# Depthwise 1/3/5 convolution with projection and residual on one core: the set-up of weights and statistics is dealt out anew among the engines

## The reference

```python
xd = concatenate([x[:, :, 0::2, 0::2], x[:, :, 0::2, 1::2], x[:, :, 1::2, 0::2], x[:, :, 1::2, 1::2]], axis=1)  # (8,128,32,32)
feats = concatenate([dwconv(xd, w1, 1), dwconv(xd, w3, 3), dwconv(xd, w5, 5)], axis=1)                       # depthwise, (8,384,32,32)
y = einsum('bchw,oc->bohw', feats, w_proj)            # 384 -> 128 channels, then back to 32 channels of 64x64
# the whole: x + conv(group_norm(x)), with 32 groups of one channel each
```

## Time and profile before

| | |
|---|---|
| median of 3 runs | 139.71 us (139.51 to 141.06) |
| profiled execution, whole | 139.66 us |
| profiled execution, span from first to last instruction | 137.8 us |
| busy PE, DVE, ACT, POOL | 92%, 90%, 79%, 85% of the span |
| granted TensorE clock, mean | 0.99 |

### The profile page before, as it was taken

How to read it: one execution, slowest core, us unless ns; L and a number is a source line. 1 busy time by engine, 2 the same in 40 slices (tenths; PEclk the granted TensorE clock), 3 DMA queues, 4 the chain that set the end, 5 groups by cost and what they waited for, 6 DMA issues and landing times.

```text
span 137.8 us, 1549 instructions
## 1 busy us (share of the span) xinstructions
PE 126.6 (92%) x508; PEld 94.8 (69%) x508; DVE 123.9 (90%) x152; ACT 109.1 (79%) x111; POOL 117.6 (85%) x88
## 2 busy tenths in 40 slices
PE   5896999999999999999999999999999999999620
PEld 5673787877876777777786777687767678577300
DVE  6659799999999999999999999999999999999660
ACT  2259989999999999999999999999999995140000
POOL 6261899999999999999999999999999999999500
PEclk9999999999999999999999999999999999999996
DMA  3999999971025008098988957795779577496596
GB/s 75 273 259 197 195 204 201 182 148 20 2 57 105 0 2 164 5 112 133 193 102 94 190 110 76 76 189 125 76 76 186 128 76 76 87 153 69 116 201 140
DMA packets 35847, 16.78 MB, mean 122 GB/s; under 512 B 34048, under 2 KB 34176, under 8 KB 35456
## 3 DMA queue, kind: packets, MB, share of 16 engines
q0 software_dynamic: 1488, 7.04, 38.0%
q1 hardware_dynamic: 32720, 9.18, 35.8%
q10 hardware_dynamic: 1632, 0.48, 1.8%
HBM read 5.46 MB, written 4.19 MB: 70 GB/s over the span
## 4 chain that ended last, share of the span: by engine, by line
DVE 76%; PE 12%; DMA 3%; issue 3%; ACT 1%; DVEq 1%; ACTq 0%
DVE ACC L602 48%; PE YP L675 10%; DVE ACC L606 7%; DVE ACC L594 7%; DVE F L612 6%; DVE st L492 3%; DMA wp_sb<-in_L_conv_w_proj_dram 3%; PE YP L726 1%; DVE weff L543 1%; DVE stp L498 1%; ACT HI L387 1%; DVEq L97 1%; ACT weff L379 1%; DVE X L636 0%; PE YP L657 0%
## 5 line engine op out<-in xcount | busy, mean ns | idle before, releaser
L317 POOL TENSOR_TENSOR RING_SUM<-RING_SUM,PROD 128x900 f32<-128x900 f32 (+1 forms) x45 | 92.6, 2065 | 3.4
L602 DVE SCALAR_TENSOR_TENSOR ACC<-G,coef,ACC 128x930 f32<-128x930 f32 (+1 forms) x59 | 70.4, 1194 | 1.8
L435 ACT ACTIVATE PROD<-G,coef 128x900 f32<-128x900 f32 (+1 forms) x45 | 44.7, 1057 | 0.0
L675 PE MATMUL YP<-HI,wlo 128*128 128x512 f32 (+1 forms) x144 | 38.3, 419 | 0.0
L675 PE MATMUL YP<-HI,whi 128*128 128x512 f32 (+1 forms) x144 | 36.4, 404 | 1.5 <-DVE HI L570 0.9
L675 PE MATMUL YP<-LO,whi 128*128 128x512 f32 (+1 forms) x144 | 36.9, 407 | 0.0
L675 PEld LDWEIGHTS YP<-HI,wlo 128*128 128x128 f32 x144 | 27.3, 190 | 9.2 <-issue 2.9
L675 PEld LDWEIGHTS YP<-HI,whi 128*128 128x128 f32 x144 | 27.0, 190 | 9.5 <-DVE HI L570 1.4
L675 PEld LDWEIGHTS YP<-LO,whi 128*128 128x128 f32 x144 | 27.2, 190 | 7.7 <-issue 1.0
L397 ACT ACTIVATE G<-X,nbias,rstd 64x1024 f32<-64x1024 f32 x16 | 21.1, 1318 | 0.9 <-DVE nbias L510 0.6
L418 ACT ACTIVATE Y<-YP 64x1024 f32<-64x1024 f32 x14 | 15.3, 1095 | 4.5 <-PE YP L726 4.3
(11 more groups left out here) (62 smaller groups left out, 61.0 us busy)
## 6 DMA issues: line engine op xcount, KB each, us to landing
X<-in_x_dram SPq DMA_DIRECT2D x16, 256.0 KB, 5.9
LO<-G POOLq DMA_DIRECT2D x7, 543.0 KB, 5.3
X<-Y POOLq DMA_DIRECT2D x6, 512.0 KB, 7.2
out_dram<-X SPq DMA_DIRECT2D x12, 256.0 KB, 4.1
out_dram<-X SPq DMA_DIRECT2D x6, 128.0 KB, 3.6
XS<-in_x_dram SPq DMA_DIRECT2D x2, 256.0 KB, 4.2
XS<-in_x_dram SPq DMA_DIRECT2D x1, 512.0 KB, 6.9
out_dram<-X ACTq DMA_DIRECT2D x2, 128.0 KB, 3.3
```

The costliest lines, as they stand in the source:

```text
L317: pool.tensor_tensor(dst, dst, prod(b, k), ALU.add).then_inc(prod_added, 1)
L435: act.activation(prod(b, k), g_tap(b, POOL_OF[b][k + 1]), ACT.Copy, scale=of5(POOL_OF[b][k + 1])).then_inc(prod_ready, 1)
L602: dve.scalar_tensor_tensor(part(ACC, tap), g_tap(b, tap), of5(tap), part(ACC, tap), ALU.mult, ALU.add).then_inc(acc_step, 1)
L675: mm = nc.tensor.matmul(dst, w[:, n, :], src, start=start, stop=False, skip_group_check=True)
```

## The change

ACT instead of DVE permutes `wp`, in the order 2, 1, 0. Part 0 is transposed into a corner of `ACC` and copied later. PE's coefficient matmul comes right behind the transposes. ACT does all its six scales ahead of the high part of image 0; before, three of them and a copy stood between its pieces. On DVE one addition of weights goes ahead of `part_variance(0)`, and `spread` for image 1 moves there from POOL. On POOL a scale goes ahead of the first power, and each `wlo` waits for one cast more than its own and no longer for all three. The entries of `between`, `COMBINE_AT` and `INV_STD_AT` for images 2 to 7 move one to three places back.

```diff
-WARM = (7, 2, 2, 9)
+WARM = (7, 4, 1, 10)
-COMBINE_AT = {(0, 8): (1, 1, 2), (1, 0): (2, 2, PAIRS)}
+COMBINE_AT = {(0, 8): (1, 1, 2), (1, 1): (2, 2, PAIRS)}
-INV_STD_AT = {(0, 2): (3, 2, 3), (1, 2): (4, 3, COLS)}
+INV_STD_AT = {(0, 3): (3, 2, 3), (1, 2): (4, 3, COLS)}
...
+        W1_PS = ACC[:, 0:P // PW, :].rearrange("p r c -> p (r c)")
+        def wt_ps(k):
+            return WT_PS[:, k * P:(k + 1) * P] if k > 0 else W1_PS
...
-            inv_std(1, 0, 1)
             pool.wait_ge(wpT_ready, 1)
             pool.wait_ge(coef_copied, 1)
             for n in range(ACT_SCALED, N_INNER):
+                if n == ACT_SCALED + 1:
+                    inv_std(1, 0, 1)
                 pool.tensor_scalar(weff[:, n, :], wpT[:, 2, :], of5(INNER[n]), None, ALU.mult).then_inc(pool_scaled, 1)
-            pool.wait_ge(whi_ready, CHUNKS)
             for k in range(CHUNKS):
+                pool.wait_ge(whi_ready, min(k + 2, CHUNKS))
...
-                if k == 0:
-                    pool.wait_ge(part_stats, 5)
-                    pool.tensor_tensor(spread[:, 1, :, :], stp[:, 1, None, :].to_broadcast([P, PARTS, STATS]),
...
-            act.wait_ge(wt_ready, 1)
+            act.wait_ge(wp_loaded, 16)
+            for k in (2, 1, 0):
+                act.activation(wp_ph[:, k, :].rearrange("p (j i c) -> p j i c", j=2, i=2),
+                               wp_sb[:, k * P:(k + 1) * P].rearrange("p (i j c) -> p j i c", i=2, j=2),
+                               ACT.Copy).then_inc(permuted, 1)
+            act.wait_ge(wt_ready, 2)
             copy_wpT(2)
+            copy_wpT(1)
             act.wait_ge(coef_ready, 1)
             act.activation(coef[:, :], COEF_PS, ACT.Copy).then_inc(coef_copied, 1)
-            copy_wpT(1)
...
-            scale_w5(0, CHUNK)
+            scale_w5(0, ACT_SCALED)
...
             high_half(0, TOP, 0, hi_top)
-            scale_w5(CHUNK, ACT_SCALED)
-            copy_wpT(0)
             high_half(TOP, PH, 0, hi_bottom)
             high_half(TOP, PH, 1, hi_ready)
+            act.wait_ge(wt_ready, 3)
+            copy_wpT(0)
             normalise(0, 0, PH, g_ready)
...
-            dve.wait_ge(wp_loaded, 16)
-            for k in range(3):
-                permute(wp_ph[:, k, :], wp_sb[:, k * P:(k + 1) * P])
...
-            part_variance(0)
+            spread_parts(0)
             dve.wait_ge(wpT_ready, 2)
             dve.wait_ge(coef_copied, 1)
-            add_w3(0, 1, 2)
+            add_w3(0)
+            part_variance(0)
+            add_w3(1, 2)
             part_bias(0)
...
             part_bn(1, 1)
+            spread_parts(1)
...
-            for k in range(3):
-                pe.wait_ge(permuted, k + 2)
-                mm = nc.tensor.transpose(WT_PS[:, k * P:(k + 1) * P], wp_ph[:, k, :], ident[:, :])
-            mm.then_inc(wt_ready, 1)
+            for n, k in enumerate((2, 1, 0)):
+                pe.wait_ge(permuted, n + 1)
+                nc.tensor.transpose(wt_ps(k), wp_ph[:, k, :], ident[:, :]).then_inc(wt_ready, 1)
+            pe.wait_ge(ident_permuted, 1)
+            pe.wait_ge(w_loaded, 48)
+            nc.tensor.matmul(COEF_PS, ident_ph[:, :], w_sb[:, :], start=True, stop=True).then_inc(coef_ready, 1)
...
                     if b == 0 and n % CHUNK == 0:
+                        if n == 0:
+                            sum_parts(1)
                         pe.wait_ge(wlo_ready, n // CHUNK + 1)
-                        if n == CHUNK:
-                            sum_parts(1)
```

More of the change, by code:

```diff
@@ L160, in build @@
         const_step, pads_zero = sem("const_step"), sem("pads_zero")
+        ident_permuted = sem("ident_permuted")
         permuted, hi_top, hi_bottom = sem("permuted"), sem("hi_top"), sem("hi_bottom")
@@ L365, in copy_wpT @@
                 act.activation(wpT[:, k, :].rearrange("p (j i o) -> p j i o", j=2, i=2),
-                               WT_PS[:, k * P:(k + 1) * P].rearrange("p (i j o) -> p j i o", j=2, i=2),
+                               wt_ps(k).rearrange("p (i j o) -> p j i o", j=2, i=2),
                                ACT.Copy).then_inc(wpT_ready, 1)
-            act.wait_ge(wt_ready, 1)
+            act.wait_ge(wp_loaded, 16)
[4 more added lines that the diff above has]
+            act.wait_ge(wt_ready, 2)
             copy_wpT(2)
+            copy_wpT(1)
             act.wait_ge(coef_ready, 1)
             act.activation(coef[:, :], COEF_PS, ACT.Copy).then_inc(coef_copied, 1)
-            copy_wpT(1)
             act.wait_ge(wpT_ready, 1)
@@ L468, in _ @@
         def _(dve):
-            def permute(dst, src):
-                dve.tensor_copy(dst.rearrange("p (j i c) -> p j i c", j=2, i=2),
-                                src.rearrange("p (i j c) -> p j i c", i=2, j=2)).then_inc(permuted, 1)
             dve.memset(LO[:, SLOTS - 1, :].bitcast(F32), 0.0).then_inc(low_zero, 1)
@@ L483, in _ @@
             dve.wait_ge(const_step, 3)
-            permute(ident_ph[:, :], ident[:, :])
+            dve.tensor_copy(ident_ph[:, :].rearrange("p (j i c) -> p j i c", j=2, i=2),
+                            ident[:, :].rearrange("p (i j c) -> p j i c", i=2, j=2)).then_inc(ident_permuted, 1)
             dve.tensor_reduce(mask[:, :], ident[:, :].rearrange("p (c k) -> p k c", k=PARTS), mybir.AxisListType.X,
@@ L550, in cast_w, with spread_parts @@
                 dve.tensor_copy(whi[:, taps, :], weff[:, taps, :]).then_inc(whi_ready, 1)
-            dve.wait_ge(wp_loaded, 16)
-            for k in range(3):
-                permute(wp_ph[:, k, :], wp_sb[:, k * P:(k + 1) * P])
+            def spread_parts(b):
+                dve.wait_ge(part_stats, 3 + 2 * b)
+                dve.tensor_tensor(spread[:, b, :, :], stp[:, b, None, :].to_broadcast([P, PARTS, STATS]),
+                                  mask[:, :, None].to_broadcast([P, PARTS, STATS]), ALU.mult).then_inc(spread_done, 1)
             part_bn(0, 0)
             part_bn(0, 1)
-            dve.wait_ge(part_stats, 3)
-            dve.tensor_tensor(spread[:, 0, :, :], stp[:, 0, None, :].to_broadcast([P, PARTS, STATS]),
-                              mask[:, :, None].to_broadcast([P, PARTS, STATS]), ALU.mult).then_inc(spread_done, 1)
-            part_variance(0)
+            spread_parts(0)
             dve.wait_ge(wpT_ready, 2)
             dve.wait_ge(coef_copied, 1)
-            add_w3(0, 1, 2)
+            add_w3(0)
+            part_variance(0)
+            add_w3(1, 2)
             part_bias(0)
@@ L617, in add_tap @@
                                              ALU.mult, ALU.add).then_inc(f_ready, 1)
-            between = {(0, 1): lambda: part_variance(1), (0, 2): lambda: part_bias(1), (0, 3): lambda: (bn(1), aggregate(1)),
-                       (0, 4): lambda: (variance(1, 1, 2), bn(2), aggregate(2)), (0, 5): lambda: bias(1, 1, 2),
-                       (0, 6): lambda: (bn(3), aggregate(3)), (0, 7): lambda: variance(2, 2, PAIRS),
-                       (0, 9): lambda: bias(2, 2, PAIRS)}
+            between = {(0, 0): lambda: part_variance(1), (0, 2): lambda: part_bias(1), (0, 3): lambda: (bn(1), aggregate(1)),
+                       (0, 5): lambda: (variance(1, 1, 2), bn(2), aggregate(2)), (0, 6): lambda: bias(1, 1, 2),
+                       (0, 8): lambda: (bn(3), aggregate(3)), (1, 0): lambda: variance(2, 2, PAIRS),
+                       (1, 2): lambda: bias(2, 2, PAIRS)}
             for b in range(B):
@@ L737, in _ @@
                 keep_warm(ident[:, :], P)
-            pe.wait_ge(w_loaded, 48)
-            nc.tensor.matmul(COEF_PS, ident_ph[:, :], w_sb[:, :], start=True, stop=True).then_inc(coef_ready, 1)
             pe.wait_ge(low_zero, 1)
```

1 line of the change is left out of this document (removed).

## The result

The changed kernel takes 143.28 us (median of 6 runs, 141.94 to 143.55), the kernel before beside it 140.12 (6 runs, 139.36 to 141.16): a ratio of 1.0201, 95% interval 1.0160 to 1.0243. Forecast were 141.2 and a range of 139.0 to 142.0. The profiled execution took 143.36, its span is 141.6: 3.7 and 3.8 more than before.

What follows compares the result with a forecast made beforehand. It took POOL's chain through `add_x` of image 5 and the last stores, almost level with DVE's, to bound the end. POOL's 1.5 delay was added to the profiled 139.66, giving 141.2 us; range 139.0 to 142.0.

Steps and rivals of the forecast that it cites:

- What bounds the kernel: At the end, DVE's chain and POOL's, through `add_x` of image 5 and eight stores, finish almost together; POOL must gain too.
- The 10.1 us of stores: From the landing of `add_x` of image 5 to the end of the span: eight stores back to back, 10.1 us.
- The variance of images 4 to 7: Now behind image 1's first tap at 37.7; POOL's last power waits until 39.9, 1.5 later than before.
- DVE's wait for POOL's power of image 1: Between the first taps of images 0 and 1, two DVE waits, 0.22 and 0.16, for POOL's power and PE's matmul go.
- The first tap gains 0.6: In the set-up, DVE's first tap starts at 15.5 instead of 16.11; at worst no gain, at best 1.5.
- The coefficient at 6.78: In PE's set-up, the coefficient matmul starts at about 6.78, after the last weight load lands at 6.74.
- Two more fillers at 0.51: On PE ahead of the statistics, two added fillers cost 0.51, so `sum_parts(0)` starts at 8.06, 1.24 later.
- rival 3: In the set-up, slow fillers (1.9 for four) give 142.1, or DVE additions held by POOL some 142 or more; chance 0.12.
- By the row nothing is added: In the set-up, `wlo` on POOL beside DVE's last additions costs nothing, as taps run beside POOL's sums at 1.194.
- Rivals 1, 2 and 4: 1: quicker set-up, 140.3, 0.17; 2: tail not tied to `add_x`, 139.3, 0.13; 4: POOL's wait absent or cheap, 138.5, 0.08.
- what the set-up gains is lost in POOL's wait: On POOL, the 1 us gained in set-up only lengthens its wait for the variance of images 4 to 7.

Runs made afterwards that it cites:

- addx_early: The changed kernel with only `add_x` of image 5 one sum earlier in POOL's list; 141.58 us, ratio 1.0072.
- old_addx_early: The kernel before with only `add_x` of image 5 one sum earlier in POOL's list; 138.59 us, ratio 0.9894.
- old_setup_new_tables: The kernel before with only the changed tables of the statistics for images 2 to 7, set-up untouched; 141.95 us, ratio 1.0123.
- wlo_apart: The changed kernel with POOL's `wlo` waiting for all three casts, the second also for DVE's `spread`; 143.38 us, ratio 1.0232.
- set_up_pool_old: The changed kernel with all tables, `wlo` and `spread` of image 1 as in the kernel before; 140.24 us, ratio 1.0005.
- fillers_first: The changed kernel with two of PE's fillers ahead of the coefficient matmul and two behind the statistics' matmul; 142.41 us, ratio 1.0161.

## Why the prediction was wrong: right about the end and the variance, wrong about the set-up

**What bounds the kernel: right.** The chain of waits named DVE before and PE after; SP's wait for `add_x` of image 5 was the true releaser in both. addx_early and old_addx_early show it by moving nothing else. The 10.1 us of stores were 9.9.

**The variance of images 4 to 7: right.** The stretch from first tap to first tap was forecast 1.2 shorter than 23.4 and was 22.03, 1.35 shorter. From the first tap of image 1 to POOL's power I had 2.2 and it is 2.12. Counted from the first tap, the step holds within 0.2. old_setup_new_tables shows that it costs 1.2% alone. One term in it is not proven by that: I let DVE's wait for POOL's power of image 1 go. In wlo_apart, whose first tap (15.61) is the one that I forecast, DVE stands 1.03 for that power, the stretch is 23.16 and the last power comes at 40.89, not 39.9. Part of that wait is the edit's, which holds POOL's `wlo` back; whether it would be there with the first tap at 15.5 and `wlo` as changed no run shows.

**The set-up, "The first tap gains 0.6": the step that failed.** It lost 2.30 (18.41 for 16.11), outside its bounds of nothing to 1.5. In an execution with short filler passes it is still 17.35, 1.24 lost. Its terms:
- The coefficient at 6.78: 7.18, 0.40 more. The load landed 0.3 later than in the profile before, and PE started behind it.
- Two more fillers at 0.51, the stretch to the statistics 1.28: it took 2.26, 0.98 more. Here the slow spacing of rival 3 came true, in four of seven profiles with this list; I gave it 0.12. My arguments against it were no use. That PE had idled 0.57 without slowing was taken from a profile in which the passes had already become short (0.61 for four, from 5.64). And the granted clock is 1.00 over slow passes as well (rows in the last section). The price was in my own rows: eight passes at the spacing of the earlier trace rows are 1.9.
- "By the row nothing is added": 1.46 were added. The row was misread. I called the taps instructions "with two inputs from SBUF", but both kernels declare `ACC` with `ps`, in PSUM, so a tap reads only `G` from SBUF; that taps and sums leave each other alone (1.195 for a tap in the changed kernel, 1.194 before) says nothing of an addition, which reads `wpT` and `weff`, both in SBUF. The pair that was needed was in the trace of the kernel before, in the timelines of DVE and POOL:

```profile
9.05 0.34 DVE L543 SCALAR_TENSOR_TENSOR weff<-wpT,coef,weff 128x128 f32<-128x128 f32 x1
9.17 1.02 POOL L335 TENSOR_SCALAR weff<-wpT,coef 128x128 f32<-128x128 f32 x1
```

POOL's three scales there take 0.61, 1.02 and 0.60; the long one starts inside one addition of DVE (9.05 to 9.39) and runs beside the next (9.31 to 9.65).

The Trainium skill says in "SBUF — State Buffer", section "Who interferes with whom", that a DVE instruction with two inputs in SBUF contends with a GpSimd instruction that reads SBUF, and that the one that comes second is blocked for the whole of the other. The two held instructions agree: each started second and ended just after the `wlo` that it ran beside (0.15 and 0.07), and the addition is back at 0.35 in set_up_pool_old and wlo_apart and `spread` at 0.21 in wlo_apart, where they are kept apart. The taps, with one input in SBUF, are no case of it. Not every pair agrees: in the kernel before, two additions start inside POOL's scale of 8.57 to 9.18, at 8.78 and 9.05, and take 0.35 and 0.34. So the rule shows where to look, and here it held for POOL's `wlo` and not for its scale; why is open.

**The rivals.** Rival 3 came true in both of its parts, the first not quite as described: the passes did not fall back to the slow spacing, those ahead of the wait were long already (0.69 for two transposes at 5.25). I had let the two stand as alternatives, 142.1 for the one and "some 142 or more" for the other, and then ended the range at 142.0, below both prices. They add: `nbias` 1.45 late and 1.46 of held instructions make the first tap 15.5 + 2.91 = 18.41. POOL's power at 42.56, 4.14 later than before, makes 139.66 + 4.14 = 143.8 by my sum; 0.1 was made good ahead of `add_x` and 0.3 behind it, which leaves the 143.36 of the profiled execution. Rivals 1, 2 and 4 are refuted: statistics later, end tied to `add_x`, POOL's wait there.

**Cover that was missed.** I wrote that what the set-up gains is lost in POOL's wait. What it loses is not covered: the variance hangs on DVE, and DVE on the set-up. From the first tap to POOL's last power are 24.15 in the changed kernel and 24.14 in fillers_first, whose first tap is 1.55 sooner. A bound of "nothing" for a loss was the error of the range, not only of the value.

## What to carry to other kernels

Look for the one transfer that the last stores wait for and follow it to the engine that issues it; the chain of waits may name another engine. If work is moved behind a step on one engine, look at who waits for it on the others, and move their place in the list with it. Where a late load or a wait is put ahead of warming passes, cost those passes at the slow spacing as well, and take the price of DVE instructions beside GpSimd's from rows whose operands lie in the same memories; the program says which tiles are in SBUF and which in PSUM. A single line, `ADD_X_AT[(7, 3)] = 5` in the kernel before, beat both kernels by 1% and more: with a list of sums ahead of a transfer on which the end depends, try the transfer one sum sooner.
